# Projections of q, k and v in three fp16 products from split operands, in place of fp32 products

## The chip, the cores and the metric

One NeuronCore of a Trainium2 chip runs the whole program in one launch. The metric is the device time of one execution in microseconds; the median of three executions of the kernel before is 2715.98 us (2710.8 to 2716.86).

## The reference

Two layers run on x of shape (2, 256, 64, 64), that is 2 batches, 256 channels, 4096 positions. The change touches only the first line of the first layer.

```python
# layer 0: attention over 8 heads of 32 channels
qkv = einsum('oc,bchw->bohw', w_qkv, x)            # w_qkv is (768, 256)
q, k, v = split(qkv, 3, axis=1)                    # each (2, 8, 32, 4096)
scores = einsum('bhdi,bhdj->bhij', q, k) / sqrt(32)
out = einsum('bhij,bhdj->bhdi', softmax(scores), v)
x = einsum('oc,bchw->bohw', w_proj, out) + x
# layer 1: a non-local block with a one-channel-set query
g_x = maxpool2(conv1x1(x, g_w, g_b)); theta = conv1x1(x[:, :64]); phi = maxpool2(conv1x1(x[:, 64:]))
y = softmax(theta^T phi) g_x
x = batchnorm(conv1x1(y, W_w, W_b)) + x
```

## The kernel before, in words

Everything stays in one loop over the two batches (`Fori(0, B)`). The program is divided into blocks: in each block every engine has its own straight list of instructions, the engines meet at the block's end, and semaphores set the order within it. Nothing is scheduled by a planner; the order written is the order run.

X holds the batch as fp32, 128 partitions by CT = 2 halves of the channels by N = 4096 positions. A chunk is CH = 512 positions of both halves, so there are NC = 8 chunks and a chunk of X is 128 x 1024 elements.

`layer0(b)` treats the heads in NG = 2 groups of 4 heads (g = 0, 1). For each group it has a projection block (L234 to L342) and an attention block (L361 to L530). So the program runs the projection block four times: g = 0 and 1 of each batch. In the block of g = 0, SyncE also loads X in 8 DMAs, one for each chunk (L336).

The projection block has two parts.

- **The q/k part** has NU = 16 units, u = 0 to 15. Before the change a unit is `k, c = divmod(u, NC)`: first the 8 chunks of q, then the 8 chunks of k. For a unit PE makes two fp32 matmuls with 512 columns (L253, one for each half of the channels; the trace holds two records for each fp32 matmul), ACT writes the high fp16 part of 16 times the result (L284) and squares it into `sq` (L288), DVE writes the low part (L305). Two units later PE sums the squares over each head (`norms`, L242) and DVE takes their maximum (`largest`, L299). Results go round through six PSUM banks (`slot`), so unit u waits for DVE's evacuation of unit u - 6 (`s_ev`). `norms(u - 2)` stands behind unit u in PE's list and waits for ACT's square of u - 2.
- **The V part** has 8 blocks q = 0 to 7 of four 128 x 128 results each, with the positions as stationary operand (L267): 8 fp32 matmuls of 128 columns each, 16 records. DVE evacuates the even blocks (L328), ACT the odd ones (L292), in turn (`s_ve`). After q = 3 PE transposes the product of the norms' maxima (L276), DVE reduces it and writes a flag (L320, L322), and only then evacuates block 0.

The setup block (L153 to L207) loads the weights, splits the weights of layer 1 into `cw` high and low (ACT L205, DVE L184), and prepares the batch norm's factors.

Of the kernel before, what the change touches and what calls it, by code (L numbers as in the profile page):

```python
# [1 line left out]

# [60 lines left out]
def conv_seq(nc, x, wqkv, wproj, gw, tw, pw, ww, vectors, biases, out, r_dram, r1_dram):  # L63
# [3 lines left out]
    with ExitStack() as root:  # L67
# [10 lines left out]
        def sem(ctx, name):  # L78
            return ctx.enter_context(nc.semaphore(unique(name)))
# [7 lines left out]

            return scores6[:, (i % 6) * CH:(i % 6 + 1) * CH]

        wq_sb = sb(root, "wq_sb", [128, CT, 3 * C])  # L90
        wp_sb = sb(root, "wp_sb", [128, CT, C])
        cw = [sb(root, f"cw_{n}", [128, CT, CM + CM + C], F16) for n in ("hi", "lo")]
        col = sb(root, "col", [128, CT, 8])
# [41 lines left out]
        with ExitStack() as ctx:  # L135

            cw32 = sb(ctx, "cw32", [128, CT, CM + CM + C])
            tw_sb, pw_sb, gw_sb = cw32[:, 0, 0:CM], cw32[:, :, CM:2 * CM], cw32[:, :, 2 * CM:]
            s_cw = sem(ctx, "s_cw")
            s_w = sem(ctx, "s_w")  # L140
            s_zero = sem(ctx, "s_zero")
            s_id = sem(ctx, "s_id")
            s_sq = sem(ctx, "s_sq")
            s_bn = sem(ctx, "s_bn")
            s_hd = sem(ctx, "s_hd")
            loads = [(wq_sb[:], wqkv.rearrange("(t p) o -> p t o", p=128)),
                     (wp_sb[:], wproj.rearrange("(t p) o -> p t o", p=128)),
                     (gw_sb, gw.rearrange("(t p) o -> p t o", p=128)),
                     (col[:, :, 0:6], vectors.rearrange("(t p) k -> p t k", p=128)),
# [3 lines left out]
            with nc.Block() as block:  # L153
# [17 lines left out]
                @block.vector  # L171
                def _(dve):
                    nc.vector.memset(cw32[:, :, 0:CM], 0.0).then_inc(s_zero, 1)
                    nc.vector.memset(pw_sb[:, 0, :], 0.0).then_inc(s_zero, 1)
                    nc.vector.memset(ones[:], 1.0)
                    nc.vector.memset(heads[:], 0.0).then_inc(s_hd, 1)
                    dve.wait_ge(s_hd, 1)
                    for h in range(G):
                        last = nc.vector.memset(heads[h * D:(h + 1) * D, h * D:(h + 1) * D], 1.0)
                    last.then_inc(s_hd, 1)  # L180
                    dve.wait_ge(s_hd, 2)
                    dve.wait_ge(s_w, 16 * (len(loads) + len(small)))
                    dve.wait_ge(s_cw, 1)
                    nc.vector.scalar_tensor_tensor(out=cw[1][:], in0=cw32[:], scalar=WS, in1=cw[0][:],  # L184
                                                   op0=ALU.mult, op1=ALU.subtract).then_inc(s_cw, 1)
                    dve.wait_ge(s_cw, 2)

                    nc.vector.tensor_scalar(sA[:, :, 0], col[:, :, 5], EPS, None, ALU.add).then_inc(s_bn, 1)
                    dve.wait_ge(s_bn, 1)
                    nc.vector.reciprocal(sA[:, :, 1], sA[:, :, 0]).then_inc(s_bn, 1)  # L190
                    dve.wait_ge(s_sq, 1)

                    nc.vector.tensor_tensor(sA[:, :, 1], sA[:, :, 0], col[:, :, 2], ALU.mult).then_inc(s_bn, 1)
                    nc.vector.tensor_tensor(col[:, :, 6], col[:, :, 1], col[:, :, 4], ALU.subtract).then_inc(s_bn, 1)
                    dve.wait_ge(s_bn, 4)
                    nc.vector.tensor_tensor(col[:, :, 7], col[:, :, 6], sA[:, :, 1], ALU.mult).then_inc(s_bn, 1)
                    dve.wait_ge(s_bn, 5)
                    nc.vector.tensor_tensor(sA[:, :, 2], col[:, :, 7], col[:, :, 3], ALU.add).then_inc(s_bn, 1)
                    nc.vector.tensor_scalar(sA[:, :, 3], sA[:, :, 1], 1.0 / (PS * QS), None, ALU.mult).then_inc(s_bn, 1)
                    dve.wait_ge(s_bn, 7)  # L200

                @block.scalar
                def _(act):
                    act.wait_ge(s_w, 16 * (len(loads) + len(small)))
                    nc.scalar.activation(cw[0][:], cw32[:], ACT.Copy, scale=WS).then_inc(s_cw, 1)  # L205
                    act.wait_ge(s_bn, 2)
                    nc.scalar.activation(sA[:, :, 0], sA[:, :, 1], ACT.Sqrt).then_inc(s_sq, 1)  # L207
            end_phase(ctx, [s_cw, s_w, s_zero, s_id, s_sq, s_bn, s_hd])

        def layer0(b):  # L210
            with ExitStack() as ctx:
# [8 lines left out]
                for g in range(NG):  # L220

                    with ExitStack() as c2:
                        sq = [sb(c2, f"sq{k}", [128, CH], BF16) for k in range(2)]
                        nmax = sb(c2, "nmax", [128, 2 * NC])
                        bound = sb(c2, "bound", [128, 4])
                        s_st = sem(c2, "s_st")
                        s_sq = sem(c2, "s_sqr")
# [6 lines left out]
                        with nc.Block() as block:  # L234
                            @block.tensor
                            def _(pe):
# [6 lines left out]
                                                     ).then_inc(s_nm, 1)  # L243

                                for u in range(NU):
                                    k, c = divmod(u, NC)
                                    if u >= 6:
                                        pe.wait_ge(s_ev, u - 5)
                                    if g == 0 and k == 0:
                                        pe.wait_ge(s_x[c], 16)  # L250
                                    for t in range(CT):
                                        w = wq_sb[:, t, k * C + g * 128:k * C + (g + 1) * 128]
                                        last = nc.tensor.matmul(slot(u), w, X[:, t, c * CH:(c + 1) * CH],  # L253
                                                                start=(t == 0), stop=(t == CT - 1))
                                    last.then_inc(s_mm, 1)
                                    if u >= 2:
                                        norms(u - 2)

                                for q in range(JT // 4):
# [3 lines left out]
                                        pe.wait_ge(s_ev, NU + q - 5)  # L263
                                    for r in range(4):
                                        j = 4 * q + r
                                        for t in range(CT):
                                            last = nc.tensor.matmul(  # L267
                                                slot(NU + q)[:, r * 128:(r + 1) * 128], X[:, t, j * 128:(j + 1) * 128],
                                                wq_sb[:, t, 2 * C + g * 128:2 * C + (g + 1) * 128],
                                                start=(t == 0), stop=(t == CT - 1))  # L270
                                    last.then_inc(s_vm, 1)
                                    if q < 2:
                                        norms(NU - 2 + q)
# [3 lines left out]

                            @block.scalar
                            def _(act):
                                for u in range(NU):  # L280
                                    k, c = divmod(u, NC)
                                    cs = slice(c * CH, (c + 1) * CH)
                                    act.wait_ge(s_mm, u + 1)
                                    nc.scalar.activation(QK[k][:, 0, cs], slot(u), ACT.Copy, scale=QS).then_inc(s_hi, 1)  # L284
                                    if u >= 2:
                                        act.wait_ge(s_nm, u - 1)
                                    act.wait_ge(s_hi, u + 1)
                                    nc.scalar.activation(sq[u % 2][:], QK[k][:, 0, cs], ACT.Square).then_inc(s_sq, 1)  # L288
                                for q in range(1, JT // 4, 2):
                                    act.wait_ge(s_vm, q + 1)  # L290
                                    act.wait_ge(s_ve, q)
                                    nc.scalar.copy(V[:, 4 * q:4 * q + 4, :].rearrange("p j n -> p (j n)"), slot(NU + q)  # L292
                                                   ).then_inc(s_ve, 1)

                            @block.vector
                            def _(dve):
# [2 lines left out]
                                    nc.vector.tensor_reduce(nmax[:, u:u + 1], (psO, psL)[u % 2], AX.X, ALU.max).then_inc(s_nx, 1)  # L299

                                for u in range(NU):
                                    k, c = divmod(u, NC)
                                    cs = slice(c * CH, (c + 1) * CH)
                                    dve.wait_ge(s_hi, u + 1)
                                    nc.vector.scalar_tensor_tensor(  # L305
                                        out=QK[k][:, 1, cs], in0=slot(u), scalar=QS, in1=QK[k][:, 0, cs],
                                        op0=ALU.mult, op1=ALU.subtract).then_inc(s_ev, 1)
                                    if u >= 2:
                                        largest(u - 2)
# [1 line left out]
                                largest(NU - 1)  # L311
                                dve.wait_ge(s_nx, NU)

                                nc.vector.tensor_reduce(bound[:, 0:2], nmax[:].rearrange("p (k c) -> p k c", k=2),
                                                        AX.X, ALU.max).then_inc(s_b, 1)
                                dve.wait_ge(s_b, 1)
                                nc.vector.tensor_tensor(bound[:, 2:3], bound[:, 0:1], bound[:, 1:2], ALU.mult
# [6 lines left out]
                                for q in range(0, JT // 4, 2):  # L324
                                    dve.wait_ge(s_vm, q + 1)
                                    if q:
                                        dve.wait_ge(s_ve, q)
                                    nc.vector.tensor_copy(V[:, 4 * q:4 * q + 4, :].rearrange("p j n -> p (j n)"), slot(NU + q)  # L328
                                                          ).then_inc(s_ve, 1)
# [12 lines left out]
                        end_phase(c2, s_x + [s_mm, s_ev, s_hi, s_st, s_sq, s_nm, s_nx, s_vm, s_ve, s_b])  # L342

                    with ExitStack() as c2:
                        P = sb(c2, "P", [128, RING * G, CH])
# [769 lines left out]
```

## Time and profile before

| | us |
|---|---|
| median of three executions | 2715.98 |
| the profiled execution | 2723.91 |
| its span in the trace | 2722.2 |
| PE busy | 2559.6 (94%) |
| ACT busy | 2223.8 (82%) |
| DVE busy | 2162.6 (79%) |
| GpSimd busy | 216.0 (8%) |
| fp32 matmuls of q and k (L253), busy | 126.3 |
| fp32 matmuls of V (L267), busy | 59.5 |

The profiled execution is one run of its own, 7.9 us above the median. Busy times are sums over records; matmul records overlap in part because their ends are modelled, so what counts for PE is the distance between starts. The granted clock is shown as a share of 2.4 GHz: 1.00 is 2.4 GHz and 0.50 is 1.2 GHz.

### The profile page before, as it was taken

To read this page: it belongs to the slowest core of one execution; us is meant where nothing else is said; L and a number is where in the kernel's file an instruction comes from. 1 tells how busy PE (TensorE), PEld (TensorE's weight loads), DVE (VectorE), ACT (ScalarE), POOL (GpSimd) and SP (SyncE) were. 2 spreads that over 40 slices of the span, in tenths; PEclk is the share of its full clock that TensorE was granted. 3 is DMA by queue.
4 is the path that set the end of the run, shared out by engine and by line. 5 is a ranking of instruction groups with operands and counts; after the bars stand their busy time and mean duration, and the time that the engine had idled before them with its cause. 6 is when DMAs were issued, how large, how long until landed. Compare 5 with 4: busy or idle time off the path is not lost. (4 is left out here: it accounts for less than half of the span.)

```text
span 2722.2 us, 57541 instructions
## 1 busy us (share of the span) xinstructions
PE 2559.6 (94%) x24666; PEld 747.0 (27%) x24666; DVE 2162.6 (79%) x1414; ACT 2223.8 (82%) x2490; POOL 216.0 (8%) x364
## 2 busy tenths in 40 slices
PE   7999999989999999598979999999899999995999
PEld 4222222242222222243442222222422222222434
DVE  3899999948999999576538999999489999995864
ACT  4999999939999999137439999999399999991474
POOL 0010000000100000011000100000000000000100
PEclk9999999999999999899989999999999999998999
DMA  2555555505555555201115555555055655552011
GB/s 83 109 127 127 121 125 125 125 17 109 125 125 125 125 125 125 82 11 47 42 68 109 127 127 121 125 125 125 17 109 128 128 122 123 127 123 82 11 51 42
DMA packets 57016, 271.97 MB, mean 100 GB/s; under 512 B 13920, under 2 KB 15008, under 8 KB 27680
## 3 DMA queue, kind: packets, MB, share of 16 engines
q0 software_dynamic: 32256, 234.90, 40.0%
q1 hardware_dynamic: 24480, 33.16, 3.6%
q8 instruction: 198, 3.24, 0.5%
q14 instruction: 82, 0.67, 0.1%
HBM read 22.88 MB, written 8.68 MB: 12 GB/s over the span
## 5 line engine op out<-in xcount | busy, mean ns | idle before, releaser
L488 DVE TENSOR_TENSOR acc<-acc,P 128x2048 f32<-128x2048 f32 x704 | 1613.2, 2292 | 85.2 <-ACT P L457 18.0
L457 ACT ACTIVATE P<-scores 128x1536 f32<-128x1536 f32 x1024 | 1593.5, 1556 | 0.0
L381 PE MATMUL psOL<-P,V 128*32 128x512 f32 (+1 forms) x8960 | 1075.2, 568 | 1.4 <-ACT P L457 1.4
L372 PE MATMUL psOL<-Q,K 32*128 32x512 f16 x3072 | 845.0, 381 | 27.5 <-ACT P L456 16.2
L372 PE MATMUL scores<-Q,K 32*128 32x512 f16 x9216 | 851.4, 381 | 0.0
L456 ACT ACTIVATE P<-psOL 128x512 f32<-128x512 f32 x1024 | 710.7, 694 | 39.0 <-PE scores L372 39.0
L372 PEld LDWEIGHTS psOL<-Q,K 32*128 32x128 f16 x3072 | 207.5, 93 | 988.5 <-ACT P L456 857.1
L381 PEld LDWEIGHTS psOL<-P,V 128*32 128x32 f32 x8960 | 196.6, 108 | 475.1 <-issue 439.2
L512 POOL DMA_DIRECT2D accD<-P x192 | 165.2, 861 | 1417.5 <-ACT P L457 682.7
L372 PEld LDWEIGHTS scores<-Q,K 32*128 32x128 f16 x9216 | 220.5, 93 | 0.0
L253 PE MATMUL scores<-X,wq_sb 128*128 128x512 f32 x256 | 126.3, 623 | 44.4 <-DMA X<-in_x 30.1
L1035 DVE SCALAR_TENSOR_TENSOR Pl<-O,Ph 128x1536 f16<-128x1536 f32 (+1 forms) x48 | 75.8, 1580 | 65.0 <-ACT Ph L1008 63.1
L488 DVE TENSOR_TENSOR acc<-P 128x2048 f32<-128x2048 f32 x32 | 73.4, 2293 | 65.3 <-PE psOL L391 35.2
L1001 ACT ACTIVATE O<-scores 128x1536 f32<-128x1536 f32 (+1 forms) x48 | 62.4, 1300 | 71.0 <-PE scores L936 71.0
L746 PE MATMUL scores<-O,wp_sb 128*128 128x512 f32 x128 | 64.8, 656 | 49.8 <-DVE O L703 49.8
L735 ACT ACTIVATE Yh<-X 128x512 f16<-128x512 f32 x32 | 20.1, 630 | 107.4 <-DVE X L723 107.4
L948 PE MATMUL psOL<-Ph,GTh 128*128 128x512 f16 x256 | 97.0, 379 | 0.0
L948 PE MATMUL psOL<-Ph,GTl 128*128 128x512 f16 x256 | 97.0, 379 | 0.0
L948 PE MATMUL psOL<-Pl,GTh 128*128 128x512 f16 x256 | 97.0, 379 | 0.0
L253 PEld LDWEIGHTS scores<-X,wq_sb 128*128 128x128 f32 x256 | 51.0, 201 | 103.9 <-issue 71.7
L305 DVE SCALAR_TENSOR_TENSOR Q<-scores,Q 128x512 f16<-128x512 f32 x32 | 22.1, 692 | 68.7 <-ACT Q L284 68.7
L509 POOL DMA_DIRECT2D accD<-P x32 | 18.0, 562 | 689.4 <-ACT P L457 403.4
(113 smaller groups left out, 1505.6 us busy)
## 6 DMA issues: line engine op xcount, KB each, us to landing
accD<-P POOLq DMA_DIRECT2D x224, 1024.0 KB, 7.3
X<-in_x SPq DMA_DIRECT2D x16, 512.0 KB, 7.0
R<-att_inv SPq DMA_DIRECT2D x32, 256.0 KB
out<-res SPq DMA_DIRECT2D x32, 256.0 KB, 2.1
R<-pool_inv SPq DMA_DIRECT2D x2, 2048.0 KB, 7.3
TB<-TA SPq DMA_DIRECT2D x2, 512.0 KB, 4.5
wq_sb<-in_w_qkv SPq DMA_DIRECT2D x1, 768.0 KB, 4.4
Ls<-L SPq DMA_DIRECT2D x32, 8.0 KB
```

Source lines behind the costliest of these rows:

```text
L253: last = nc.tensor.matmul(slot(u), w, X[:, t, c * CH:(c + 1) * CH], start=(t == 0), stop=(t == CT - 1))
L305: nc.vector.scalar_tensor_tensor(out=QK[k][:, 1, cs], in0=slot(u), scalar=QS, in1=QK[k][:, 0, cs], op0=ALU.mult, op1=ALU.subtract).then_in ...
L372: last = nc.tensor.matmul(dst[h], K[rows, kp, j * 128:(j + 1) * 128], Q[rows, qp, cs], start=(n == 0), stop=(n == 2))
L381: last = nc.tensor.matmul(both[h * D:(h + 1) * D, lo:hi], V[:, j, h * D:(h + 1) * D], P[:, r + h, lo:hi], start=(j == 0), stop=(j == JT - 1))
L456: nc.scalar.activation(P[:, r, :], lead, ACT.Exp, scale=SCORE).then_inc(s_exp, 1)
L457: nc.scalar.activation(P[:, r + 1:r + G, :], bank[n % 2].rearrange("p (u n) -> p u n", n=CH), ACT.Exp, scale=SCORE).then_inc(s_exp, 1)
L488: nc.vector.tensor_tensor(acc[:], old, P[:, r:r + G, :], ALU.add).then_inc(s_add, 1)
L512: nc.gpsimd.dma_start(dst, src, accum_op=ALU.add).then_inc(s_dma, 16)
L746: last = nc.tensor.matmul(slot(u), wp_sb[:, k, t * 128:(t + 1) * 128], O[:, k, c * CH:(c + 1) * CH], start=(k == 0), stop=(k == CT - 1))
L948: last = nc.tensor.matmul(psOL[:, t * CH:(t + 1) * CH], w[:, m, ts], v[:, p, m, :], start=(n == 0), stop=(n == 3 * MT - 1))
L1001: nc.scalar.activation(P32[:, p, ms, :], bank[o % 2][:, 0:SZ[k] * CH].rearrange("p (u n) -> p u n", n=CH), ACT.Exp, scale=SCORE1).then_inc ...
L1035: nc.vector.scalar_tensor_tensor(out=Pl[:, p, ms, :], in0=P32[:, p, ms, :], scalar=PS, in1=Ph[:, p, ms, :], op0=ALU.mult, op1=ALU.subtract ...
```

## The change

The weights of q, k and v are split once, in the setup block, into a high and a low fp16 part of 256 times their value: ACT casts the high part (`wq[0]`), DVE subtracts for the low part (`wq[1]`), both ahead of the same work for layer 1.

In each projection block X is split as well, chunk by chunk, into Xh and Xl, the high and low fp16 parts of 16 times X. ACT casts the high part (`high(c)`), GpSimd multiplies the chunk by 16 into a scratch tile and subtracts Xh from it. Both groups of heads do this anew. Every fp32 product becomes three fp16 products: high times high, low weight times high X, high weight times low X. A unit of q or k has 6 matmuls of 512 columns, a V block 24 matmuls of 128 columns. The units are now `c, k = divmod(u, 2)`: q and k of chunk 0, then of chunk 1, and so on. The evacuations scale by 1/256 or 1/4096.

```diff
@@ setup block
+                    dve.wait_ge(s_wq, 1)
+                    nc.vector.scalar_tensor_tensor(out=wq[1][:], in0=wq32[:], scalar=WS, in1=wq[0][:],
+                                                   op0=ALU.mult, op1=ALU.subtract).then_inc(s_wq, 1)
+                    dve.wait_ge(s_wq, 2)
                     dve.wait_ge(s_cw, 1)
...
                     act.wait_ge(s_w, 16 * (len(loads) + len(small)))
+                    nc.scalar.activation(wq[0][:], wq32[:], ACT.Copy, scale=WS).then_inc(s_wq, 1)
                     nc.scalar.activation(cw[0][:], cw32[:], ACT.Copy, scale=WS).then_inc(s_cw, 1)
@@ projection block
+                        Xh = sb(c2, "Xh", [128, CT, N], F16)
+                        Xl = sb(c2, "Xl", [128, CT, N], F16)
+                        Xs = [sb(c2, f"Xs{k}", [128, CT, CH]) for k in range(2)]
@@ tensor
                                 for u in range(NU):
-                                    k, c = divmod(u, NC)
+                                    c, k = divmod(u, 2)
                                     if u >= 6:
                                         pe.wait_ge(s_ev, u - 5)
-                                    if g == 0 and k == 0:
-                                        pe.wait_ge(s_x[c], 16)
-                                    for t in range(CT):
-                                        w = wq_sb[:, t, k * C + g * 128:k * C + (g + 1) * 128]
-                                        last = nc.tensor.matmul(slot(u), w, X[:, t, c * CH:(c + 1) * CH],
-                                                                start=(t == 0), stop=(t == CT - 1))
+                                    outs = slice(k * C + g * 128, k * C + (g + 1) * 128)
+                                    for n, (wp, xp) in enumerate(((0, Xh), (1, Xh), (0, Xl))):
+                                        if n == 0:
+                                            pe.wait_ge(s_xh, c + 1)
+                                        if n == 2:
+                                            pe.wait_ge(s_xl, c + 1)
+                                        for t in range(CT):
+                                            last = nc.tensor.matmul(slot(u), wq[wp][:, t, outs],
+                                                                    xp[:, t, c * CH:(c + 1) * CH],
+                                                                    start=(n == 0 and t == 0), stop=(n == 2 and t == CT - 1))
...
-                                        for t in range(CT):
+                                        for n, (t, xp, wp) in enumerate(itertools.product(range(CT), (0, 1), (0, 1))):
+                                            if xp and wp:
+                                                continue
                                             last = nc.tensor.matmul(
-                                                slot(NU + q)[:, r * 128:(r + 1) * 128], X[:, t, j * 128:(j + 1) * 128],
-                                                wq_sb[:, t, 2 * C + g * 128:2 * C + (g + 1) * 128],
-                                                start=(t == 0), stop=(t == CT - 1))
+                                                slot(NU + q)[:, r * 128:(r + 1) * 128],
+                                                (Xh, Xl)[xp][:, t, j * 128:(j + 1) * 128],
+                                                wq[wp][:, t, 2 * C + g * 128:2 * C + (g + 1) * 128],
+                                                start=(n == 0), stop=(t == CT - 1 and xp == 1))
@@ scalar
+                                def high(c):
+                                    cs = slice(c * CH, (c + 1) * CH)
+                                    if g == 0:
+                                        act.wait_ge(s_x[c], 16)
+                                    nc.scalar.activation(Xh[:, :, cs], X[:, :, cs], ACT.Copy, scale=QS).then_inc(s_xh, 1)
+
+                                high(0)
+                                high(1)
                                 for u in range(NU):
-                                    k, c = divmod(u, NC)
+                                    c, k = divmod(u, 2)
                                     cs = slice(c * CH, (c + 1) * CH)
                                     act.wait_ge(s_mm, u + 1)
-                                    nc.scalar.activation(QK[k][:, 0, cs], slot(u), ACT.Copy, scale=QS).then_inc(s_hi, 1)
+                                    nc.scalar.activation(QK[k][:, 0, cs], slot(u), ACT.Copy, scale=1.0 / WS).then_inc(s_hi, 1)
+                                    if k == 0 and c + 2 < NC:
+                                        high(c + 2)
@@ gpsimd
+                                for c in range(NC):
+                                    cs = slice(c * CH, (c + 1) * CH)
+                                    pool.wait_ge(s_xh, c + 1)
+                                    if c >= 2:
+                                        pool.wait_ge(s_xl, c - 1)
+                                    nc.gpsimd.tensor_scalar(Xs[c % 2][:], X[:, :, cs], QS, None, ALU.mult).then_inc(s_xs, 1)
+                                    pool.wait_ge(s_xs, c + 1)
+                                    nc.gpsimd.tensor_tensor(Xl[:, :, cs], Xs[c % 2][:], Xh[:, :, cs], ALU.subtract
+                                                            ).then_inc(s_xl, 1)
```

ACT's list at the start of the projection block of g = 0, before (Q and K are the tiles of q and k, `scores` the PSUM banks):

```order
L284 ACT_TABLE_LOAD
L284 ACTIVATE Q<-scores 128x512
L288 ACTIVATE sq<-Q 128x512
L284 ACTIVATE Q<-scores 128x512
L288 ACTIVATE sq<-Q 128x512
L284 ACTIVATE Q<-scores 128x512
```

The same place now:

```order
L305 ACT_TABLE_LOAD
L305 ACTIVATE Xh<-X 128x2x512 x2
L313 ACTIVATE Q<-scores 128x512
L305 ACTIVATE Xh<-X 128x2x512
L319 ACTIVATE sq<-Q 128x512
L313 ACTIVATE K<-scores 128x512
L319 ACTIVATE sq<-K 128x512
L313 ACTIVATE Q<-scores 128x512
```

Two casts of X stand ahead of everything, and one cast stands in the middle of each of the next six chunks, ahead of that q unit's square.

PE's list from the last unit of k into the V part, before:

```order
L253 MATMUL scores<-X,wq_sb 128x512 x2
L242 MATMUL psOL<-sq,heads 128x512
L267 MATMUL scores<-wq_sb,X 128x128 x8
L242 MATMUL psOL<-sq,heads 128x512
L267 MATMUL scores<-wq_sb,X 128x128 x8
L242 MATMUL psOL<-sq,heads 128x512
L267 MATMUL scores<-wq_sb,X 128x128 x16
L276 MATMUL psOL<-ident,bound 1x128
L267 MATMUL scores<-wq_sb,X 128x128 x32
```

The same place now (the three rows of L287 come eight times in a V block):

```order
L270 MATMUL scores<-Xh,wq_hi 128x512 x2
L270 MATMUL scores<-Xh,wq_lo 128x512 x2
L270 MATMUL scores<-Xl,wq_hi 128x512 x2
L256 MATMUL psOL<-sq,heads 128x512
L287 MATMUL scores<-wq_hi,Xh 128x128
L287 MATMUL scores<-wq_lo,Xh 128x128
L287 MATMUL scores<-wq_hi,Xl 128x128
```

The norms and the transposition keep their places behind the units; 2 fp32 matmuls of a unit have become 6 fp16 ones, and 8 of a V block have become 24.

## Rows read from the trace of the kernel before

**Rows 1.** The page's groups: line, engine, operation, shapes, count | busy us, mean ns | idle before

```profile
L457 ACT ACTIVATE P<-scores 128x1536 f32<-128x1536 f32 x1024 | 1593.5, 1556 | 0.0
```

**Rows 2.** Timeline of the first projection stage: start us, length us, engine, line, operation

```profile
16.21 7.46 PE L253 MATMUL scores<-X,wq_sb 128*128 128x512 f32 x12 [16.21 <-DMA X<-in_x]
...
33.17 0.38 PE L242 MATMUL psOL<-sq,heads 128*128 128x512 bf16 x1
33.37 0.60 ACT L284 ACTIVATE Q<-scores 128x512 f16<-128x512 f32 x1 [0.61 <-PE scores L253]
33.39 1.88 PE L253 MATMUL scores<-X,wq_sb 128*128 128x512 f32 x4
34.06 0.63 ACT L288 ACTIVATE sq<-Q 128x512 bf16<-128x512 f16 x1
```

**Rows 3.** Timeline of the V part of the first projection stage

```profile
48.85 1.95 PE L267 MATMUL scores<-wq_sb,X 128*128 128x128 f32 x16
...
56.53 7.31 PE L267 MATMUL scores<-wq_sb,X 128*128 128x128 f32 x64
57.11 0.67 DVE L328 COPY V<-scores 128x512 f32<-128x512 f32 x1
57.87 0.59 ACT L292 COPY V<-scores 128x512 f32<-128x512 f32 x1 [7.72 <-DVE V L328]
58.57 0.69 DVE L328 COPY V<-scores 128x512 f32<-128x512 f32 x1 [0.78 <-PE scores L267]
...
63.88 0.58 ACT L292 COPY V<-scores 128x512 f32<-128x512 f32 x1 [2.48 <-PE scores L267]
```

**Rows 4.** Timeline of PE in the second projection stage

```profile
560.19 6.83 PE L253 MATMUL scores<-X,wq_sb 128*128 128x512 f32 x12 [7.03 <-issue]
...
592.20 1.95 PE L267 MATMUL scores<-wq_sb,X 128*128 128x128 f32 x16
```

**Rows 5.** Timeline of PE in layer 1

```profile
1291.59 0.38 PE L948 MATMUL psOL<-Pl,GTh 128*128 128x512 f16 x1
1291.80 0.38 PE L948 MATMUL psOL<-Ph,GTh 128*128 128x512 f16 x1
```

**Rows 6.** Groups of ACT and DVE by shape, whole span

```profile
L1008 ACT ACTIVATE Ph<-O 128x1536 f16<-128x1536 f32 x32 | 47.5, 1483 | 2.3
L1008 ACT ACTIVATE Ph<-O 128x1024 f16<-128x1024 f32 x16 | 16.9, 1057 | 0.5
L1035 DVE SCALAR_TENSOR_TENSOR Pl<-O,Ph 128x1536 f16<-128x1536 f32 x32 | 56.2, 1758 | 40.8 <-ACT Ph L1008 39.0 <-DMA R<-pool_inv 1.9
```

**Rows 7.** Timeline of GpSimd in layer 1, first batch

```profile
1159.42 1.80 POOL L774 MEMSET TB<- 64x2048 f32 x1 [69.40 <-POOLq L108]
1161.17 0.52 POOL L775 MEMSET PB<- 64x512 f32 x1
...
1214.03 0.22 POOL L907 TENSOR_SCALAR m<-mx 128x1 f16<-128x1 f32 x1 [0.66 <-DVE mx L1023]
1214.31 0.19 POOL L910 CAST stat<-m 128x1 f32<-128x1 f16 x1
```

**Rows 8.** Timeline of the setup

```profile
7.89 0.84 ACT L205 ACTIVATE cw_hi<-cw 128x768 f16<-128x768 f32 x1 [5.87 <-DMA cw<-in_phi_w]
8.88 0.96 DVE L184 SCALAR_TENSOR_TENSOR cw_lo<-cw,cw_hi 128x768 f16<-128x768 f32 x1 [7.16 <-ACT cw_hi L205]
12.46 4.29 SPq L336 DMA_DIRECT2D X<-in_x  x8
```

**Rows 9.** Groups of weight loads by shape

```profile
L267 PEld LDWEIGHTS scores<-wq_sb,X 128*128 128x128 f32 x512 | 59.4, 192 | 1.8 <-issue 1.3
L948 PEld LDWEIGHTS psOL<-Ph,GTh 128*128 128x128 f16 x256 | 25.1, 98 | 30.2
```

**Rows 10.** Stretches: us, busy us of PE, PEld, DVE, ACT, POOL, granted clock, DMA

```profile
560.00:562.00 2.00, 1.81 (x2) 0.84 (x3) 0.00 (x0) 0.00 (x0) 0.00 (x0) 0.50 0.05 12
...
1140.00:1160.00 20.00, 13.33 (x32) 5.18 (x31) 14.06 (x20) 5.04 (x8) 0.57 (x1) 1.00 0.17 57
```

More of the change, by code:

```diff
@@ L1 @@
+import itertools
 from contextlib import ExitStack
@@ L88, in slot @@
             return scores6[:, (i % 6) * CH:(i % 6 + 1) * CH]
-        wq_sb = sb(root, "wq_sb", [128, CT, 3 * C])
+        wq = [sb(root, f"wq_{n}", [128, CT, 3 * C], F16) for n in ("hi", "lo")]
         wp_sb = sb(root, "wp_sb", [128, CT, C])
@@ L138, in conv_seq @@
             tw_sb, pw_sb, gw_sb = cw32[:, 0, 0:CM], cw32[:, :, CM:2 * CM], cw32[:, :, 2 * CM:]
+            wq32 = sb(ctx, "wq32", [128, CT, 3 * C])
             s_cw = sem(ctx, "s_cw")
+            s_wq = sem(ctx, "s_wq")
             s_w = sem(ctx, "s_w")
@@ L145, in conv_seq @@
             s_hd = sem(ctx, "s_hd")
-            loads = [(wq_sb[:], wqkv.rearrange("(t p) o -> p t o", p=128)),
+            loads = [(wq32[:], wqkv.rearrange("(t p) o -> p t o", p=128)),
                      (wp_sb[:], wproj.rearrange("(t p) o -> p t o", p=128)),
@@ L207, in _ @@
                     nc.scalar.activation(sA[:, :, 0], sA[:, :, 1], ACT.Sqrt).then_inc(s_sq, 1)
-            end_phase(ctx, [s_cw, s_w, s_zero, s_id, s_sq, s_bn, s_hd])
+            end_phase(ctx, [s_cw, s_wq, s_w, s_zero, s_id, s_sq, s_bn, s_hd])
         def layer0(b):
@@ L223, in layer0 @@
                         sq = [sb(c2, f"sq{k}", [128, CH], BF16) for k in range(2)]
+                        Xh = sb(c2, "Xh", [128, CT, N], F16)
+                        Xl = sb(c2, "Xl", [128, CT, N], F16)
+                        Xs = [sb(c2, f"Xs{k}", [128, CT, CH]) for k in range(2)]
                         nmax = sb(c2, "nmax", [128, 2 * NC])
+                        s_xs = sem(c2, "s_xs")
+                        s_xh = sem(c2, "s_xh")
+                        s_xl = sem(c2, "s_xl")
                         bound = sb(c2, "bound", [128, 4])
@@ L291, in _ @@
                                     act.wait_ge(s_ve, q)
-                                    nc.scalar.copy(V[:, 4 * q:4 * q + 4, :].rearrange("p j n -> p (j n)"), slot(NU + q)
-                                                   ).then_inc(s_ve, 1)
+                                    nc.scalar.activation(V[:, 4 * q:4 * q + 4, :].rearrange("p j n -> p (j n)"), slot(NU + q),
+                                                         ACT.Copy, scale=1.0 / (QS * WS)).then_inc(s_ve, 1)
+                            @block.gpsimd
+                            def _(pool):
+                                for c in range(NC):
[7 more added lines that the diff above has]
+                                                            ).then_inc(s_xl, 1)
                             @block.vector
@@ L301, in _ @@
                                 for u in range(NU):
-                                    k, c = divmod(u, NC)
+                                    c, k = divmod(u, 2)
                                     cs = slice(c * CH, (c + 1) * CH)
@@ L305, in _ @@
                                     nc.vector.scalar_tensor_tensor(
-                                        out=QK[k][:, 1, cs], in0=slot(u), scalar=QS, in1=QK[k][:, 0, cs],
+                                        out=QK[k][:, 1, cs], in0=slot(u), scalar=1.0 / WS, in1=QK[k][:, 0, cs],
                                         op0=ALU.mult, op1=ALU.subtract).then_inc(s_ev, 1)
@@ L312, in _ @@
                                 dve.wait_ge(s_nx, NU)
-                                nc.vector.tensor_reduce(bound[:, 0:2], nmax[:].rearrange("p (k c) -> p k c", k=2),
+                                nc.vector.tensor_reduce(bound[:, 0:2], nmax[:].rearrange("p (c k) -> p k c", k=2),
                                                         AX.X, ALU.max).then_inc(s_b, 1)
@@ L327, in _ @@
                                         dve.wait_ge(s_ve, q)
-                                    nc.vector.tensor_copy(V[:, 4 * q:4 * q + 4, :].rearrange("p j n -> p (j n)"), slot(NU + q)
-                                                          ).then_inc(s_ve, 1)
+                                    nc.vector.tensor_scalar(V[:, 4 * q:4 * q + 4, :].rearrange("p j n -> p (j n)"), slot(NU + q),
+                                                            1.0 / (QS * WS), None, ALU.mult).then_inc(s_ve, 1)
                                 dve.wait_ge(s_b, 4)
@@ L341, in _ @@
                                     sp.wait_ge(s_st, 16)
-                        end_phase(c2, s_x + [s_mm, s_ev, s_hi, s_st, s_sq, s_nm, s_nx, s_vm, s_ve, s_b])
+                        end_phase(c2, s_x + [s_xh, s_xl, s_xs, s_mm, s_ev, s_hi, s_st, s_sq, s_nm, s_nx, s_vm, s_ve, s_b])
                     with ExitStack() as c2:
```

## The prediction

> **What bounds the kernel now.** I read the page's groups first, then the timeline of the four projection blocks, then the groups by shape for the cost of each new operation. The largest group, ACT's exponentials of the attention blocks, is 1593.5 us [rows 1], and none of that is edited. What is edited is four blocks of about 48 us each, and a piece of setup. In the first block PE starts at 16.21 and goes to the V part at 48.85, so the q/k part lasts 32.6 us; in the second it lasts from 560.19 to 592.20, 32.0 us [rows 2 to 4]. I take 32.3. Both figures hold a start at half clock. After that a unit costs 1.93 us (eight units between 33.39 and 48.85 [rows 2, 3]), of which 0.22 is the norm (33.17 to 33.39 [rows 2]). PE has no gap there while ACT works 0.60 + 0.63 of each 1.93 us [rows 2], so PE bounds the q/k part. The V part lasts from 48.85 to the end of ACT's last copy, 63.88 + 0.58 = 64.46 [rows 3]: 15.6 us, again PE's, 64 records in 7.31 us [rows 3]. So the blocks are PE-bound and an ACT with room takes new work; the question is who is last afterwards.
>
> **PE's share of the q/k part.** The new unit has 6 fp16 matmuls of 512 columns. Starts of such matmuls, each with its own weights, are 1291.80 - 1291.59 = 0.215 us apart [rows 5] (rounded in the rows). Six are 1.29 us, with the norm 1.51 instead of 1.93, 24.2 us for 16 units instead of 30.9. The 6.7 us are only an offer.
>
> **ACT's share.** Now ACT also casts 128 x 1024 for each chunk: 1.057 us by the same cast from fp32 in SBUF [rows 6]. For a chunk that is 2 x (0.60 + 0.63) + 1.06 = 3.52 us. Gaps: the square at 34.06 starts 0.09 behind the evacuation's end, 33.37 + 0.60 [rows 2]; I take 0.21 for the five operations of a chunk, so 3.73, more than PE's 3.02. Laid out from the block's start: cast 0 ends at 1.06, GpSimd gives Xl of chunk 0 at 4.6 (below), two matmuls at half clock take 0.86, and ACT begins its first evacuation at 5.5. From there to the square of unit 13 (PE's V part needs the norm of 13 behind unit 15) it has 14 x 1.23 + 6 x 1.06 = 23.6, 1.5 of gaps, and I add 0.8 for the second unit, which PE makes at half clock. That is 31.4; one handover, the norm, and some slack of the last unit make 32.0. Against 32.3 the q/k part gains 0.3.
>
> **GpSimd's share.** It has two operations for each chunk of 1024 elements. Neither is in the trace. Writing alone [rows 7] took 0.52 us for 512 and 1.80 for 2048 elements, so 0.83 us for each 1000 and 0.95 for 1024; an operation on one element took 0.22; the next one starts 0.06 behind it. For the multiplication the bounds are 0.95 (one stream) and 1.9 (reading and writing one after the other), and I take 1.1, one stream and the fixed cost. For the subtraction they are 0.95 and 2.75 (three streams in turn plus 0.2), and I take 2.2, two operands in turn with a little more. With two handovers of 0.07 a chunk is P = 3.45 us, with ends at 2.0 and 4.8. GpSimd starts at 1.13, the last Xl is there at 1.1 + 8P, and behind it PE has two matmuls, a norm, a whole unit and a norm, 2.3 us. GpSimd's line is thus 3.4 + 8P = 31.0, one microsecond under ACT's. From P = 3.57 on it is the last.
>
> The Trainium skill, "GPSIMD Engine Reference", section "Performance versus the Vector engine", gives 4497 ns for a two-input addition of 2048 fp32 elements, about 2.6 cycles an element, and calls one-input work nearly line rate; it advises against GpSimd for elementwise work. As an estimate from that page, P would be 0.95 + 2.25 + 0.14 = 3.3, and ACT would still be last. No row of this trace shows a two-input operation on GpSimd.
>
> **The V part.** A block is 24 matmuls of 128 columns, each with its own weights of 128 x 128. A fourth of the 215 ns is 54; the fp32 stream pays 7.31 / 64 = 114 ns for a record of two passes of 54 [rows 3], so some 6 ns over its columns. I take 60 ns, 1.44 us a block in place of 1.9. Bounds: 54 ns below; above 114, if a record of one pass costs as much as one of two. PE's eight blocks, two norms and the transposition make 11.5 + 0.43 + 0.15 = 12.1. But the evacuations begin late: block 3 ends at 4 x 1.44 + 0.43 = 6.2, the flag takes 0.8, and then eight evacuations in turn, 58.57 - 57.11 = 1.46 for two [rows 3], take 5.84. The last ends at 12.85. So the evacuations, hidden now, set the end, and the V part goes from 15.6 to 12.85, a gain of 2.75.
>
> **The setup.** ACT casts 128 x 1536 more, 1.48, and DVE subtracts as much, 1.76 [rows 6]. Today ACT's cast runs at 7.89, DVE's subtraction from 8.88 to 9.84 [rows 8]. Then: ACT to 9.37, DVE from 9.5 to 11.26, and DVE's old subtraction (0.96, its ACT part long done) to 12.26. All behind moves by 2.4 us, the load of X too, which is issued at 12.46 [rows 8]. Once.
>
> **Edits at nothing.** The V evacuations get a scale and keep their engines: they read the same bank, and 0.58 and 0.60 are ACT's times without and with a scale [rows 2, 3]. The new order of q and k costs nothing by itself; it is what lets a chunk of X serve two units. GpSimd gets an instruction ahead of its first multiplication that sets it up; in the block of g = 0 it lies beside the load of X, 12.46 to 16.21 [rows 2, 8]. Without that cover it would be late by its own length, in two blocks. Three more semaphores to clear are under 0.1 us a block.
>
> **The sum.** A block gains 0.3 + 2.75 = 3.05, four gain 12.2, the setup costs 2.4: 9.8 us less. The profiled execution's 2723.91 would become 2714.1. It lies 7.9 above the median of the runs shown, 2715.98, and I make the forecast for the median: 2706.
>
> **Rivals.**
>
> GpSimd sets the pace, slower than before. One mechanism in one place: PE's last two matmuls of each unit wait for Xl, and all eight chunks go through GpSimd in a row. It speaks for it that the margin to ACT is 0.12 us a chunk, and that both prices are bounds around unseen operations; against it, that writing goes at 0.83 us for 1000 elements. At P = 4.2, a little over half way from my value to the upper bound, the q/k part is 3.4 + 33.6 = 37.0, 4.7 more than now; less 2.75 in V that is 1.95, times four and with the setup 10.2 more: 2726. It decides from P = 3.86 (four blocks lose what the setup leaves); each tenth beyond costs 3.2 us. At the upper bound, 4.8, it is 3.4 + 38.4 - 32.3 - 2.75 = 6.75 a block, 29 more, 2745.
>
> Weight loads are not hidden behind 128 columns. A load of 128 x 128 fp16 has a row of 98 ns, longer than the 54 that a matmul streams; with 512 columns it vanishes. Against it: the fp32 load is 192 ns long [rows 9] and its matmuls still follow at 114. If each matmul waited for its load, at 98 ns, a V block would be 2.35 and the part 19.4, 3.8 more than now; four times 3.5 and 2.4 make 16.4 more: 2732. The Trainium skill, "TensorE: Matmul & The Clock Gate", section "Back-to-back issue gap", gives 81 ns for such pairs of load and matmul; by that figure, as an estimate, the V part would be 16.1 and the whole 3 us slower. No row here has that form.
>
> The matmuls fall to 1.2 GHz. The block starts at 0.50 [rows 10], now with a wait between the first matmuls, and PE has idle time later. Against it: PE works 3.02 of 3.73, and a stretch with 13.33 of 20 us kept 1.00 [rows 10]. If it stayed low, a chunk would take 6.0 and a V block 2.6: about 17 and 5 more a block, 90 in all, 2806.
>
> The gains cancel. ACT has more gaps, P is near 3.8, or the matmuls of V take near 75 ns: each takes about 2 us off a block, and the kernel stays at 2715.
>
> **How the numbers follow.** My forecast has 0.47, GpSimd's pace 0.28, exposed loads 0.14, the low clock 0.03, the cancelling case 0.08. The measurement can tell about 0.2%, 5.4 us. The forecast's own range, with GpSimd at 2.0 to 3.6 and V matmuls of 54 to 68 ns, is 2699 to 2712; a small part of it is within 5.4 us. The cancelling case is all there, and parts of the two slower rivals that are mild. That gives faster 0.45, same 0.22, slower 0.33. The range from 2697 to 2737 leaves out the low clock, P near 4.8 and loads beyond 100 ns.
>
> **What would show it.** In the profile after: ACT almost without gaps in the q/k part, its casts of X at 1.06; GpSimd's two operations at 1.1 and 2.2, with GpSimd waiting for ACT; PE waiting for Xl only in the first chunks; V matmuls 60 ns apart and waits for evacuations at the end; the first load of X at 14.9. The forecast is wrong if GpSimd has no gap between chunks and PE waits for it in each, if the two operations together pass 3.7 us, or if V matmuls start 80 ns or more apart.

## The result and the profile after

The kernel with the change runs in 2746.95 us (median of four, 2743.49 to 2751.07), the kernel before in 2716.42 beside it: ratio 1.0115, 95% interval 1.0100 to 1.0129. It is 30.5 us slower, where 10 us less were forecast. The profiled execution took 2746.51 us, 0.4 below the median; the one of before lay 7.5 above its own, so the two traces differ by only 22.3 us of span.

The groups of GpSimd by shape in the profile after (line, operation, shapes, count | busy us, mean ns | idle us before) show both of its new operations:

```profile
L333 POOL TENSOR_SCALAR Xs<-X 128x1024 f32<-128x1024 f32 x32 | 88.7, 2772 | 178.5 <-ACT Xh L305 176.2
L335 POOL TENSOR_TENSOR Xl<-Xs,Xh 128x1024 f16<-128x1024 f32 x32 | 67.9, 2122 | 2.7
```

The subtraction is at 2.12 us, near the 2.2 taken. The multiplication by 16, a one-input operation that I had priced at 1.1 and bounded by 1.9, takes 2.77. A chunk costs GpSimd 5.06 us with its handovers instead of 3.45.

The timeline of two chunks in the block of g = 1, first batch (start, length, engine, line, operation, idle before and releaser; rows of the other engines are left out) shows what this does to PE:

```profile
586.53 0.61 PE L270 MATMUL scores<-Xl,wq_hi 128*128 128x512 f16 x2 [1.47 <-POOL Xl L335]
...
586.56 2.77 POOL L333 TENSOR_SCALAR Xs<-X 128x1024 f32<-128x1024 f32 x1
...
589.13 0.59 PE L270 MATMUL scores<-Xh,wq_lo 128*128 128x512 f16 x2
...
589.41 2.12 POOL L335 TENSOR_TENSOR Xl<-Xs,Xh 128x1024 f16<-128x1024 f32 x1
...
591.59 0.60 PE L270 MATMUL scores<-Xl,wq_hi 128*128 128x512 f16 x2 [1.86 <-POOL Xl L335]
591.62 2.77 POOL L333 TENSOR_SCALAR Xs<-X 128x1024 f32<-128x1024 f32 x1
...
592.24 0.60 ACT L313 ACTIVATE Q<-scores 128x512 f16<-128x512 f32 x1 [1.79 <-PE scores L270]
```

GpSimd goes from one chunk straight to the next, 591.62 - 586.56 = 5.06. PE makes the first four matmuls of the next q unit, stops, and goes on 30 ns before GpSimd starts the chunk after: it idles 1.86 us in each of these chunks (1.47 in the third one). Before, it had no gap there [rows 2]. ACT is idle too.

The beginning of the same q/k part, from the timeline of ACT:

```profile
570.24 2.01 ACT L305 ACTIVATE Xh<-X 128x1024 f16<-128x1024 f32 x2 [11.25 <-issue]
```

The timeline of PE and, in the last row, ACT, from there to the end of the V part:

```profile
571.35 1.04 PE L270 MATMUL scores<-Xh,wq_hi 128*128 128x512 f16 x2 [7.30 <-ACT Xh L305]
572.18 1.06 PE L270 MATMUL scores<-Xh,wq_lo 128*128 128x512 f16 x2
576.41 1.03 PE L270 MATMUL scores<-Xl,wq_hi 128*128 128x512 f16 x2 [3.17 <-POOL Xl L335]
...
613.78 0.38 PE L256 MATMUL psOL<-sq,heads 128*128 128x512 bf16 x1
614.00 0.22 PE L287 MATMUL scores<-wq_hi,Xh 128*128 128x128 f16 x1
614.05 0.22 PE L287 MATMUL scores<-wq_lo,Xh 128*128 128x128 f16 x1
...
625.72 0.60 ACT L323 ACTIVATE V<-scores 128x512 f32<-128x512 f32 x1 [0.89 <-DVE V L371]
```

ACT's first cast starts at 570.24 (the row holds two), the V part at 614.00: 43.76 us against 32.0 in [rows 4]. Eight times 5.06 are 40.5; the remaining 3.3 are the first cast and what PE still has to do behind the last Xl. The prediction's formula 3.4 + 8P gives 43.9. The matmuls of V stand 56 ns apart, and the V part ends at 626.32: 12.3 us against 15.6 in [rows 3]. All four blocks agree to 0.1 us.

In the setup the load of X is issued at 14.90 instead of 12.46 [rows 8], as computed:

```profile
7.89 1.48 ACT L212 ACTIVATE wq_hi<-wq 128x1536 f16<-128x1536 f32 x1 [5.88 <-DMA cw<-in_phi_w]
9.52 1.76 DVE L187 SCALAR_TENSOR_TENSOR wq_lo<-wq,wq_hi 128x1536 f16<-128x1536 f32 x1 [7.80 <-ACT wq_hi L212]
11.31 0.96 DVE L191 SCALAR_TENSOR_TENSOR cw_lo<-cw,cw_hi 128x768 f16<-128x768 f32 x1
14.90 4.34 SPq L379 DMA_DIRECT2D X<-in_x  x8
```

The account of the two traces, each block from its first work to its last V copy: 56.1 us (four times) against 48.25, 47.62, 47.61 and 48.20, 32.7 more; 2.5 in front of the first block; and 12.9 less in the four stretches between and behind the blocks, whose work no line of the change touches. Of these 12.9, 7.2 lie in the stretch behind the second block. Here is its window before (stretch, length, busy us of PE, PEld, DVE, ACT and POOL, granted clock, DMA):

```profile
607.81:1376.00 768.19, 707.88 (x6411) 206.55 (x6412) 598.87 (x412) 592.92 (x660) 62.03 (x123) 0.96 0.41 94
```

And the same stretch after:

```profile
626.32:1387.28 760.96, 700.41 (x6411) 204.88 (x6411) 598.78 (x412) 592.15 (x659) 61.40 (x123) 0.98 0.41 95
```

The mean granted clock is 0.96 before and 0.98 after. The trace's records of the clock, which the rows round, hold 55 us at the low one of its two levels before and 30 after; in the first 32 us of the stretch the granted clock is 0.79 before and 0.95 after. No run was made to test that this accounts for the 7.2 us, but the ten traces of this case, which all hold this stretch, speak for it: it is shortest, 759.3 us, with 31 us at the low level (only V in fp16 products, casts placed early) and longest, 769.8 us, with 54 (Xh kept), and over all ten it grows, with scatter, by about 0.3 us for each microsecond at the low level. For 25 us less that makes some 7.7 us, an estimate. It is a difference between two single executions, and the medians do not have it in full: 35.2 by the blocks and the setup stand against 30.5 measured (27 to 35 by the interval).

### The profile page after: what moved, and what is told of

The parts are those of the page before. It is cut to its first block and busy times, and to the rows that moved or that the text cites. A ratio compares the mean times of both kernels' runs of the same rounds, so it can differ in the third digit from the quotient of the medians.

```text
span 2744.5 us, 58469 instructions
## 1 busy us (share of the span) xinstructions
PE 2523.2 (92%) x25038; PEld 717.9 (26%) x25050; DVE 2164.2 (79%) x1415; ACT 2250.7 (82%) x2523; POOL 372.9 (14%) x428
## 5 line engine op out<-in xcount | busy, mean ns | idle before, releaser
L555 POOL DMA_DIRECT2D accD<-P x192 | 165.5, 862 | 1409.2 <-ACT P L500 749.6
L531 DVE TENSOR_TENSOR acc<-P 128x2048 f32<-128x2048 f32 x32 | 73.4, 2293 | 61.9 <-PE psOL L434 35.2
L333 POOL TENSOR_SCALAR Xs<-X 128x1024 f32<-128x1024 f32 x32 | 88.7, 2772 | 178.5 <-ACT Xh L305 176.2
L270 PE MATMUL scores<-Xl,wq_hi 128*128 128x512 f16 x128 | 42.0, 412 | 58.3 <-POOL Xl L335 58.2
L270 PE MATMUL scores<-Xh,wq_hi 128*128 128x512 f16 x128 | 43.1, 422 | 48.8 <-ACT Xh L305 48.5
```

The costliest lines, as they stand in the source:

```text
L270: last = nc.tensor.matmul(slot(u), wq[wp][:, t, outs], xp[:, t, c * CH:(c + 1) * CH], start=(n == 0 and t == 0), stop=(n == 2 and t == CT ...
L333: nc.gpsimd.tensor_scalar(Xs[c % 2][:], X[:, :, cs], QS, None, ALU.mult).then_inc(s_xs, 1)
L531: nc.vector.tensor_tensor(acc[:], old, P[:, r:r + G, :], ALU.add).then_inc(s_add, 1)
L555: nc.gpsimd.dma_start(dst, src, accum_op=ALU.add).then_inc(s_dma, 16)
```

## The experiments

Theory A: GpSimd's eight chunks in a row set the q/k part, its multiplication is the price that was wrong, and everything else in the change is a gain. Theory B: the new order, the casts in front and the waits inside a unit are the loss. Theory C: GpSimd's operations are slow because other engines use SBUF at the same time. The edits are shortened to the lines that matter.

**Without the factor 16 on X.** High and low part are taken of X itself, the factor moves into the evacuations, and GpSimd only subtracts.

```diff
-nc.scalar.activation(Xh[:, :, cs], X[:, :, cs], ACT.Copy, scale=QS)
+nc.scalar.activation(Xh[:, :, cs], X[:, :, cs], ACT.Copy)
-nc.gpsimd.tensor_scalar(Xs[c % 2][:], X[:, :, cs], QS, None, ALU.mult).then_inc(s_xs, 1)
-nc.gpsimd.tensor_tensor(Xl[:, :, cs], Xs[c % 2][:], Xh[:, :, cs], ALU.subtract)
+nc.gpsimd.tensor_tensor(Xl[:, :, cs], X[:, :, cs], Xh[:, :, cs], ALU.subtract)
-scale=1.0 / WS       # evacuations of q and k, ACT and DVE
+scale=QS / WS
-scale=1.0 / (QS * WS)   # evacuations of V, ACT and DVE
+scale=1.0 / WS
```

> The changed kernel with X split without the factor 16: ACT casts X itself, GpSimd only subtracts (2.12 us a chunk in the changed kernel), the multiplication (2.77 us) is gone and the factor goes into the evacuations. Theory A (GpSimd's eight chunks in a row set the q/k part, 5.06 us each, and nothing else is wrong with the change): a chunk costs GpSimd 2.2 us, ACT's line of about 32 us is the last again, and the kernel is at 2706 us (2700 to 2711). Theory B (the order by chunks, the casts ahead of everything and the waits between the three products cost the time by themselves): most of the loss stays, 2735 to 2745 us.

Measured: 2684.35 us beside 2715.13, ratio 0.9883 (0.9866 to 0.9899). That is 31 us faster than before and 62.6 below the changed kernel. Theory B falls: order, casts and waits are all still there. GpSimd is no longer last: in the block of g = 1 it idles about 1.0 us in nearly every chunk until ACT's cast is there, and the q/k part from the first cast is 27.4 to 28.1 us instead of 43.8. But A had 2706, and the 22 us beyond it say that my line of ACT was too long as well. The timeline of ACT in the block of g = 1:

```profile
562.88 0.58 ACT L311 ACTIVATE Q<-scores 128x512 f16<-128x512 f32 x1
563.36 1.05 ACT L303 ACTIVATE Xh<-X 128x1024 f16<-128x1024 f32 x1
564.30 0.62 ACT L317 ACTIVATE sq<-Q 128x512 bf16<-128x512 f16 x1
564.82 0.59 ACT L311 ACTIVATE K<-scores 128x512 f16<-128x512 f32 x1
565.50 0.63 ACT L317 ACTIVATE sq<-K 128x512 bf16<-128x512 f16 x1
566.03 0.58 ACT L311 ACTIVATE Q<-scores 128x512 f16<-128x512 f32 x1
```

The five operations of a chunk are 0.58 + 1.05 + 0.62 + 0.59 + 0.63 = 3.47 long, yet the next chunk begins after 566.03 - 562.88 = 3.15. Where the operand is ready, the next operation starts about 0.1 us before the last one ends; only the square behind K's evacuation, which waits for that very result, starts late. PE's chunk is 3.02, so the two are level. The trace of before had shown it, in ACT's rows at the start of attention:

```profile
66.33 0.60 ACT L456 ACTIVATE P<-psOL 128x512 f32<-128x512 f32 x1 [1.86 <-PE scores L372]
66.82 1.45 ACT L457 ACTIVATE P<-scores 128x1536 f32<-128x1536 f32 x1
68.15 0.60 ACT L456 ACTIVATE P<-psOL 128x512 f32<-128x512 f32 x1
```

66.82 is 0.11 before 66.33 + 0.60. I had added lengths and put gaps between them.

**The low part on DVE.**

```diff
+nc.vector.scalar_tensor_tensor(out=Xl[:, :, cs], in0=X[:, :, cs], scalar=QS, in1=Xh[:, :, cs],
+                               op0=ALU.mult, op1=ALU.subtract)
```

In DVE's list two low parts stand ahead of all units, and each later one ahead of the evacuation of a unit of k.

> The changed kernel with the low part of X made by DVE in one scalar_tensor_tensor of 128 x 1024 (1.23 us by the same form elsewhere), GpSimd idle. Theory A: DVE is then last, 2 x (0.69 + 0.68) + 1.23 = 3.97 us a chunk and some 0.2 of gaps, a q/k part of about 35 us instead of 42.7, so about 2716 us (2710 to 2722). Theory B: 2735 to 2745 us, as the order and the waits stay.

Measured: 2705.33, ratio 0.9963 (0.9949 to 0.9977): faster than before, with the factor 16 kept and GpSimd idle. B falls again. The size is 11 us better than A's for the same reason: on DVE, too, an operation starts up to 0.1 us before the last one ends. A chunk is 3.75 us by its timeline, from one low part of X to the next, and PE waits 0.55 us in each for the low part, so DVE is last:

```profile
567.16 1.21 DVE L333 SCALAR_TENSOR_TENSOR Xl<-X,Xh 128x1024 f16<-128x1024 f32 x1
...
570.91 1.22 DVE L333 SCALAR_TENSOR_TENSOR Xl<-X,Xh 128x1024 f16<-128x1024 f32 x1
```

**The multiplication as tensor_tensor.**

```diff
-nc.gpsimd.tensor_scalar(Xs[c % 2][:], X[:, :, cs], QS, None, ALU.mult)
+nc.gpsimd.tensor_tensor(Xs[c % 2][:], X[:, :, cs], c16[:], ALU.mult)
```

> The changed kernel with GpSimd's multiplication by 16 written as tensor_tensor with a tile full of 16 in place of tensor_scalar; same elements, same order. Theory A with a slow tensor_scalar: the multiplication takes about 2.2 instead of 2.77 us, a chunk 4.45 instead of 5.06, 0.6 x 32 chunks = 19 us less than the changed kernel, 2727 us. Theory C (the operation is slow because it shares access to SBUF with the other engines): a second two-input operation is no better, 2747 us or more.

Measured: 2733.3, ratio 1.0066 (1.0049 to 1.0083), 13.6 us below the changed kernel, where A had 19. GpSimd's groups:

```profile
L336 POOL TENSOR_TENSOR Xs<-X,c 128x1024 f32<-128x1024 f32 x32 | 75.3, 2353 | 16.3 <-ACT Xh L306 16.3
L338 POOL TENSOR_TENSOR Xl<-Xs,Xh 128x1024 f16<-128x1024 f32 x32 | 67.9, 2122 | 2.5
```

The product took 2.35 us and not 2.2. With 2.35 instead of 2.77 and less between the two operations, a chunk is 4.52 by its timeline, and the q/k part from the first cast is 39.6 (3.3 and eight times 4.52 make 39.5), four times 4.2 less. A two-input operation is faster here than the one-input one, which speaks for A and against C.

**GpSimd alone.** A block ahead of layer 0 runs its operations on four sizes while every other engine waits.

```diff
+for m in (256, 512, 1024, 2048):
+    for rep in range(2):
+        done(nc.gpsimd.tensor_scalar(tb[:, 0:m], ta[:, 0:m], QS, None, ALU.mult))
+        done(nc.gpsimd.tensor_tensor(tb[:, 0:m], ta[:, 0:m], ta[:, 0:m], ALU.mult))
+        done(nc.gpsimd.tensor_copy(tb[:, 0:m], ta[:, 0:m]))
+        done(nc.gpsimd.tensor_tensor(td[:, 0:m], ta[:, 0:m], te[:, 0:m], ALU.subtract))
+        ...
```

> The kernel before with a block of its own between setup and layer 0, in which only GpSimd works: tensor_scalar (times 16, plus 16, fp16 output), tensor_tensor and tensor_copy on 256, 512, 1024 and 2048 columns. Theory A with a slow tensor_scalar: alone it takes the same 2.77 us for 1024 columns as in the changed kernel, about 2.6 ns a column, and the subtraction 2.12. Theory C (shared access to SBUF): alone both take clearly less, 1.1 to 1.9 us for 1024 columns. The block adds some 110 us to the time, which says nothing.

Measured, groups of GpSimd (L230 times 16, L231 product, L232 copy, L234 subtraction, L235 times 16 into fp16):

```profile
L230 POOL TENSOR_SCALAR tb<-ta 128x2048 f32<-128x2048 f32 x2 | 10.7, 5366 | 0.2
L234 POOL TENSOR_TENSOR td<-ta,te 128x2048 f16<-128x2048 f32 x2 | 8.1, 4056 | 0.2
L235 POOL TENSOR_SCALAR td<-ta 128x1024 f16<-128x1024 f32 x2 | 5.5, 2774 | 0.2
L230 POOL TENSOR_SCALAR tb<-ta 128x1024 f32<-128x1024 f32 x2 | 5.5, 2769 | 0.2
L234 POOL TENSOR_TENSOR td<-ta,te 128x1024 f16<-128x1024 f32 x2 | 4.2, 2122 | 0.2
L232 POOL COPY tb<-ta 128x2048 f32<-128x2048 f32 x2 | 3.8, 1892 | 0.1
L232 POOL COPY tb<-ta 128x1024 f32<-128x1024 f32 x2 | 2.1, 1037 | 0.1
L230 POOL TENSOR_SCALAR tb<-ta 128x256 f32<-128x256 f32 x2 | 1.7, 860 | 0.2
```

Alone, tensor_scalar takes 2769 ns for 1024 columns and the subtraction 2122, what they take in the kernel. C falls. Between 1024 and 2048 columns tensor_scalar costs 2.54 ns a column, the subtraction 1.89, a copy 0.83. The copy's rate is that of the writes alone in [rows 7], from which my price had been read. Why tensor_scalar costs more than a two-input operation no run shows.

**Only V in fp16 products.** q and k stay fp32 in the old order; X is split without the factor.

```diff
+act, behind unit u:  if u % 2 == 1: high(u // 2)
+pe, ahead of the V part:  pe.wait_ge(s_xl, NC)
```

> Only V is made of three fp16 products (X split without the factor, one subtraction a chunk on GpSimd); q and k stay fp32 products in the old order. Theory A: the V part is 12.3 us instead of 15.6 as in the changed kernel, the q/k part stays at 32.3 because ACT's casts fit beside PE (1.23 + 0.53 of 1.93 us a unit), the setup costs 1 us: four times 3.3 less 1 gives 12 less, 2704 us (2700 to 2709). Theory B makes no claim on V; if the V gain does not reach the end of the block, 2716 us.

Measured: 2723.97, ratio 1.0037 (1.0024 to 1.0051), a miss by 20 us, and the fault is the experiment's. The last cast stands behind unit 15, so PE waits for the last Xl ahead of V:

```profile
48.38 0.38 PE L256 MATMUL psOL<-sq,heads 128*128 128x512 bf16 x1
52.38 0.23 PE L284 MATMUL scores<-wq_hi,Xh 128*128 128x128 f16 x1 [3.62 <-POOL Xl L326]
```

It idles 3.6 us, and in three of the blocks the V part itself then took 14.0 to 15.1 us instead of 12.3. Those three have a mean granted clock of 0.88, 0.81 and 0.81 in the V part, and where it is at the low level the matmuls stand 107 ns apart; in the block that took 12.3 us it is 1.00, after the same wait of 3.6 us. So the casts were moved:

```diff
-if u % 2 == 1: high(u // 2)
+if u in (1, 2, 4, 6, 8, 9, 11, 12): high((1, 2, 4, 6, 8, 9, 11, 12).index(u))
```

> The version with only V in fp16 products, with the eight casts of X placed behind units 1, 2, 4, 6, 8, 9, 11 and 12 instead of behind every second one up to 15, so that the last low part is there before the V part begins. Theory A: the 3.6 us that PE waited there are gone, the V part is 12.3 us, four blocks gain 3.3 each and the setup costs 1: 2704 us. If V in fp16 products brings nothing at the end of the block, 2716 us.

Measured: 2705.59, ratio 0.9961 (0.9948 to 0.9973). The V part is 12.3 us in all four blocks, so the V term exists without the rest of the change. The q/k part took 33.4 to 33.6 us in three blocks and 32.0 in the third. The casts are not the reason: all four blocks have them, and at the full clock PE goes from unit to unit in 1.93 us without a gap. The clock is: in the second block the first 5.8 us are at the low level, in the third the first 2.9, which is 1.5 us of the q/k part. The setup and the start of the first block cost 0.2 us, not 1. So the blocks' lengths and the start account for 9.8 us, the medians for 12.5 with an interval of some 3.4 to either side.

**The old order of the units.**

```diff
-c, k = divmod(u, 2)
+k, c = divmod(u, NC)
```

> The unscaled version with the units in the old order, the eight chunks of q and then the eight of k. Theory A: in the q pass a unit cannot be faster than GpSimd's 2.2 us a chunk, 17.6 us for eight, the k pass is PE's 8 x 1.51 = 12.1, with the start some 31.5 to 33 us from the first cast instead of 27.4, four times 4 to 5 more than the unscaled version: 2700 to 2704 us. Theory B (the order by chunks is itself a cost): faster than the unscaled version's 2684.

Measured on the unscaled version: 2705.33, ratio 0.9962 (0.9952 to 0.9973), 21 us above the unscaled version with the new order. The q/k part from the first cast is 31.9 to 32.4 us instead of 27.4 to 28.1. In the q pass every unit needs a new chunk, and PE waits for GpSimd, which for its part waits 0.18 us for ACT's cast at every second chunk:

```profile
566.18 0.60 PE L268 MATMUL scores<-Xl,wq_hi 128*128 128x512 f16 x2 [0.84 <-POOL Xl L329]
...
568.32 0.60 PE L268 MATMUL scores<-Xl,wq_hi 128*128 128x512 f16 x2 [0.45 <-POOL Xl L329]
```

So the order by chunks, which the prediction priced at nothing, is part of the gain once GpSimd is fast enough.

**Xh kept for the second group.**

```diff
-Xh = sb(c2, "Xh", [128, CT, N], F16)
+Xh = O[:, 1, :].bitcast(F16).rearrange("p (t n) -> p t n", t=CT)
+# casts of X only where g == 0
```

> The unscaled version with Xh kept for the second group of heads in the half of O that is not yet written, so that ACT casts nothing in the blocks of g = 1. In the unscaled version a chunk takes ACT 3.16 us and PE 3.02. Theory A: in g = 1 PE is last, 8 x 0.14 = 1.1 us less, and its first matmul comes 1.1 us earlier as it waits for no cast: two blocks, 4 us less, 2680 us. If PE rather than ACT was already the last, only the 1.1 us of the start in two blocks go, 2682 us.

Measured: 2687.89, ratio 0.9888 (0.9866 to 0.9911), not told apart from the unscaled version's 0.9883. In the trace the q/k part of the second block is 25.1 us, against 27.4 with its cast: the 2.2 us expected are there. In the fourth it is 26.5 against 27.4, with 5.5 us at the low clock at its start where the second has 2.8. Even 4.5 us in all would be within the interval.

The unscaled version, with Xh kept or not, is the best of those run: 1.2% faster than the kernel before.

## Why the prediction was wrong

- **GpSimd's share: the step that failed.** It took the multiplication at 1.1 us within "0.95 (one stream) and 1.9 (reading and writing one after the other)". It is 2.77, outside the bounds. They were made from a row that writes and computes nothing, and from one on a single element, and assumed that only streams of data cost time; the probe shows three times a copy's cost for each column. With it P is 5.06 instead of 3.45, beyond even the upper bound of 4.8, and GpSimd is last instead of ACT. The rival on the other side had this mechanism, the place and the point at which it decides (P = 3.86; redone, its sum gives 3.88); it had P = 4.2, and too small a chance. That 2745, its time at the upper bound, lies by the measured 2747 is luck in part: its P was 4.8, and at 5.06 the same sum gives 2754.
- **ACT's share: wrong by 0.6 us a chunk.** 3.73 was forecast, 3.15 measured where ACT is free to run. In the changed kernel this is hidden behind GpSimd. The likeliest case was wrong in itself by it: with ACT that fast, GpSimd's line of 31.0 us at the forecast's own P of 3.45 would have been the last, and by the prediction's formula, with 12.3 for V, the kernel would have gained 16 us, not 10 (an estimate). The unscaled version, with a P of about 2.2, gains 31.
- **PE's share: right.** A unit's six matmuls stand 0.215 us apart; PE's chunk is 3.02.
- **The V part: right.** 12.3 us against 12.85 forecast, matmuls 56 ns apart against 60, and the evacuations at the end 1.49 us for two. The rival with exposed weight loads is out: loads of 98 ns [rows 9] lie wholly behind matmuls 56 ns apart. The 81 ns of the Trainium skill ("TensorE: Matmul & The Clock Gate", "Back-to-back issue gap") does not hold here.
- **The setup: right,** 2.44 us. The instruction ahead of GpSimd's first multiplication cost nothing to be seen: in the second block the multiplication starts at 571.38, 30 ns behind the first matmul, which waits for the same cast.
- **The half clock: hidden.** In the second block the matmuls stay at 1.2 GHz, 0.43 us apart, for the first 18, until 582.2, eleven microseconds after the first one; [rows 10] had the low level there too, and in that trace it was over at 563.1, three after the first one. GpSimd's line covers it, and the stage did not stay low.
- **The sum.** With P = 5.06 in the prediction's own formula, the q/k part is 43.9 instead of 32.3 and V 12.3 instead of 15.6: 8.3 us a block, 33.2, and the setup 2.4: 35.6 more, against 30.5 measured. The blocks and the setup of the trace bear the sum out (35.2); what the medians lack of it stays open.

The estimate of 3.3 us for a chunk, in part from the Trainium skill ("GPSIMD Engine Reference", "Performance versus the Vector engine"), was no better. The 2.25 us for the subtraction, half of what that section gives for 2048 elements, is near the measured 2.12. The near line rate for one input, which the same text of the Trainium skill states under "Engine selection", holds for a copy, 0.83 ns a column, and not for tensor_scalar at 2.54. Its advice against elementwise work on GpSimd was the part to weigh more.

## What to carry to other kernels

A rate read from a row that only writes, or only copies, is no bound for an operation that computes: time the operation alone first, as one run did here, or keep it off a line whose margin (here 0.12 us a chunk) is smaller than the bounds are apart. A constant factor need not be applied by the slowest engine: fold it into an evacuation that multiplies anyway. And read an engine's rate from the distance between starts, not from the lengths of its operations.

## What the runs showed of the hardware

- GpSimd's tensor_scalar costs the same for times 16, plus 16, and fp16 or fp32 output: 2769 to 2774 ns for 128 x 1024. It is slower than a two-input operation of the same size (1893 with one operand read twice, 2122 to 2353 with two).
- fp16 matmuls of 128 columns, each with its own 128 x 128 weights, start 56 ns apart at 2.4 GHz and 107 ns apart at 1.2 GHz.
- ACT operations that wait for nothing start about 0.1 us before the one ahead has ended.
